# Routed experts run as one pipeline, and mixture stages whose shared units go first with expert choice beside the second unit

## The reference, cut to what matters

```python
# twice (stages a and c): expert choice, each of 8 experts takes its 1024 best tokens
S = sigmoid(xt @ Wg).T;  G, I = top_k(S, 1024);  ex = xt[I]
hid = gelu(einsum('ekh,ehf->ekf', ex, W1) + b1)            # FF = 1024
out = (einsum('ekf,efh->ekh', hid, W2) + b2) * G[..., None]
x = x + 0.5 * zeros.at[I].add(out)
# twice (stages d and f): each token takes 4 of 16 experts out of 2 of 4 groups, and all take the shared part
scores = softmax(x @ gate_w.T);  c = weights of the 4 chosen, 0 elsewhere
y = einsum('tei,eid,te->td', silu(x@w1) * (x@w3), w2, c)   # INTER = 128
z = silu(x @ ws1) * (x @ ws3) @ ws2                        # 2 * 128 wide
x = x + 0.5 * (y + z)
```

## Time and profile before

| what | value |
|---|---|
| time of 3 runs | 4653.36 us median (4644.17 to 4657.75) |
| profiled execution, its own time | 4639.34 us |
| its span | 4637.6 us |
| PE, DVE, ACT, POOL busy | 87%, 59%, 43%, 12% |

### The profile page before, as it was taken

How to read it: one execution, slowest core, us unless ns; L and a number is a source line. 1 busy time by engine, 2 the same in 40 slices (tenths; PEclk the granted TensorE clock), 3 DMA queues, 4 the chain that set the end, 5 groups by cost and what they waited for, 6 DMA issues and landing times. The chain is left out here.

```text
span 4637.6 us, 74096 instructions
## 1 busy us (share of the span) xinstructions
PE 4047.9 (87%) x26222; PEld 3129.6 (67%) x26222; DVE 2729.8 (59%) x5268; ACT 1988.4 (43%) x3960; POOL 566.3 (12%) x428
## 2 busy tenths in 40 slices
PE   4599949989974599968999969999999997799999
PEld 3488835555544588857888856666566664788888
DVE  4544446665645544437777756655666555577777
ACT  1555524544440555512333336555655554133332
POOL 0144321211200144210000000000000000000000
PEclk6699968999995799969999979999999999699999
DMA  3243220000003343220000020000000001000001
GB/s 113 89 93 82 30 57 6 24 20 16 24 25 100 100 85 80 29 56 11 14 10 11 6 77 6 10 11 11 1 10 10 11 6 38 18 11 14 10 14 36
DMA packets 144876, 159.23 MB, mean 34 GB/s; under 512 B 20320, under 2 KB 132704, under 8 KB 144352
## 3 DMA queue, kind: packets, MB, share of 16 engines
q1 hardware_dynamic: 117728, 113.15, 7.5%
q0 software_dynamic: 26880, 42.48, 5.0%
HBM read 105.01 MB, written 50.59 MB: 34 GB/s over the span
## 5 line engine op out<-in xcount | busy, mean ns | idle before, releaser
L1895 ACT ACTIVATE e_prob<-e_s_ps,e_small 128x512 f32<-128x512 f32 x512 | 346.7, 685 | 173.2 <-PE e_t_ps L1785 88.2
L2006 DVE TENSOR_REDUCE e_small<-e_s_ps 128x2 f32<-128x1024 f32 x256 | 313.3, 1224 | 170.8 <-PE e_s_ps L1772 166.6
L1312 ACT ACTIVATE b_pt<-b_t_ps 128x1024 f32<-128x1024 f32 (+3 forms) x256 | 180.9, 706 | 305.0 <-PE b_t_ps L1244 304.0
L1785 PE MATMUL e_t_ps<-const,e_prob 128*128 128x128 f32 x2048 | 267.9, 274 | 9.5 <-ACT e_pt L1884 5.3
L1806 PE MATMUL e_z_ps<-e_pt,e_v 128*64 128x512 f32 x1024 | 275.5, 617 | 0.4 <-DVE e_zf L2086 0.4
L1984 POOL TENSOR_TENSOR e_wide<-e_small,const 128x512 f32<-128x512 f32 x64 | 66.5, 1039 | 1708.4 <-DVE e_small L2079 1708.4
L1785 PEld LDWEIGHTS e_t_ps<-const,e_prob 128*128 128x128 f32 x2048 | 234.1, 141 | 55.8 <-issue 22.5
L1495 DVE TENSOR_REDUCE b_small<-b_s_ps 128x2 f32<-128x1024 f32 (+3 forms) x256 | 209.8, 820 | 85.1 <-PE b_s_ps L1223 81.1
L942 DVE SCALAR_TENSOR_TENSOR d_xs<-d_o_ps,d_coef,d_xs 128x256 f32<-128x256 f32 x576 | 238.1, 476 | 1.3 <-PE d_o_ps L62 1.3
L942 DVE SCALAR_TENSOR_TENSOR f_xs<-f_o_ps,f_coef,f_xs 128x256 f32<-128x256 f32 x576 | 238.1, 476 | 1.3 <-PE f_o_ps L62 1.3
L60 PE MATMUL f_h_ps<-f_x_hi,f_w_hi 128*128 128x512 f32 x576 | 227.5, 395 | 0.0
(11 more groups left out here) (540 smaller groups left out, 11757.0 us busy)
## 6 DMA issues: line engine op xcount, KB each, us to landing
ae_raw<-w_dram SPq DMA_DIRECT2D x16, 1024.0 KB
ce_raw<-w_dram SPq DMA_DIRECT2D x16, 1024.0 KB
d_raw<-m_dram SPq DMA_DIRECT2D x54, 128.0 KB, 2.2
f_raw<-m_dram SPq DMA_DIRECT2D x54, 128.0 KB, 2.2
b_xs<-x_dram SPq DMA_DIRECT2D x9, 512.0 KB, 3.8
ar_xs<-x_dram SPq DMA_DIRECT2D x8, 512.0 KB, 9.3
x_dram<-ar_xs SPq DMA_DIRECT2D x8, 512.0 KB, 7.6
rows_dram<-ar_xn POOLq DMA_DIRECT2D x8, 512.0 KB, 4.7
```

What stands on the lines that cost most here:

```text
L1312: act.activation(pt[:, kt % 2, a, :, 0:width], t_ps[:, :, 0:width], ACT.Exp).then_inc(p_ready, 1)
L1785: last = pe.transpose(t_ps[:, h, kt * P:(kt + 1) * P], prob[:, bank_of(s) + h, kt * P:(kt + 1) * P], ident)
L1895: act.activation(prob[:, at], s_ps[:, at], ACT.Exp, bias=nmx[:, at:at + 1], accum_out=sums[:, buf, h * QT + s:h * QT + s + 1]).then_inc(p_ ...
L2006: dve.tensor_reduce(nmx[:, at:at + 2], s_ps[:, at:at + 2], AX.X, ALU.max, negate=True).then_inc(mx_ready, 1)
```

## The change

**Experts.** down follows its up by two steps (LAG = 2), across experts too, so `h_hi` and `h_lo` have 4 buffers and the x parts 2. The next expert's transposes are spread over steps 8, 10, 12 and 14, its weights are split in 8 pieces of twice the size, and the last half's bias and gate come in the third step of the next expert. Gathers signal in pairs, and GpSimd issues the gather of expert e+2 between the two scatters of expert e.

**Mixture.** The unit order is rotated: the two shared units, whose coefficient is the constant 0.5, are units 0 and 1. Transposes and logits of group g run between the steps of unit 0, out of the second half of `o_ps`; the logits are copied to SBUF. The choice of experts is cut in eight parts, and DVE runs one behind each step of unit 1. The low part `h_lo` is made on GpSimd instead of DVE in all 144 steps. The weights of unit 1 are loaded behind the tokens.

```diff
 def ffn0_experts(nc, tag, rows, x_out, w1, b1, w2, b2, const, idx):
+        LAG, RING = 2, 4
+        SPLIT_AT = (2, 3, 4, 5, 7, 9, 11, 13)
+        TURN_AT = (8, 10, 12, 14)
...
+            def gather_next(e):
+                gp.wait_ge(t_ready, e * PAIRS)
+                gp.wait_ge(gates_done, e)
+                gather(e)
...
             for e in range(E0):
-                body(e, e + 1 < E0)
-            gp.wait_ge(added, E0 * 16 * CC)
+                scatter(e, 0)
+                if e + 2 < E0:
+                    gather_next(e + 2)
+                scatter(e, 1)
...
             def body(e, b, more):
                 for n in range(N):
                     up(e, b, n)
-                    if n >= 1:
-                        down(e, b, n - 1)
-                if more:
-                    transposes(e + 1)
-                down(e, b, N - 1)
+                    if n >= LAG:
+                        down(e, b, n - LAG)
+                    elif later(e):
+                        down(e - 1, 1 - b, N + n - LAG)
+                    if isinstance(e, int) and e == 0 and n in (0, 2):
+                        transposes(0, 2 + n // 2)
+                    if more and n in TURN_AT:
+                        transposes(e + 1, TURN_AT.index(n))
...
                     act.activation(hid[:, n % 2], h_ps[:, n % 2], ACT.Gelu, bias=b1_sb[:, b, f:f + 1]).then_inc(hid_ready, 1)
-                    if more:
-                        split_w(e + 1, 1 - b, n)
...
+                    if more and n in SPLIT_AT:
+                        split_w(e + 1, 1 - b, SPLIT_AT.index(n))
...
+                    if more and n in TURN_AT:
+                        split_x(e + 1, 1 - b, TURN_AT.index(n))
+                    if n == LAG and later(e):
+                        scale_y(e - 1, 1 - b, 1)
+                    if n == FC + LAG:
                         scale_y(e, b, 0)
...
 def moe(nc, tag, x_in, x_out, gate_w, w1, w3, w2, const):
...
             def weights(u, b):
+                at = (u + E1) % UNITS
...
             def down(b, g, first):
                 n = first + g
                 pe.wait_ge(hid_lo, n + 1)
-                if isinstance(n, int) and n < 2:
-                    pe.wait_ge(soft_in, 2)
-                else:
+                head = isinstance(n, int) and n < NG
+                if head and n:
+                    pe.wait_ge(o_used, n)
+                elif isinstance(n, int) and NG <= n < NG + 2:
+                    pe.wait_ge(o_used, NG)
+                    pe.wait_ge(lg_out, 1)
+                elif not head:
                     pe.wait_ge(o_used, n - 1)
...
+            for k in range(KC):
+                transposes(0, k)
+            for g in range(NG):
+                more = g + 1 < NG
+                if more:
+                    transposes(g + 1, 0)
+                else:
+                    pe.wait_ge(x_lo_done, NG * KC)
+                logits(g)
+                if more:
+                    transposes(g + 1, 1)
+                up(0, g, 0)
+                if g >= 1:
+                    down(0, g - 1, 0)
...
+        @block.gpsimd
+        def _(gp):
+            def unit(b, first, u, more):
+                for g in range(NG):
+                    gp.wait_ge(hid_hi, first + (g + 1))
+                    gp.tensor_tensor(h_lo[:, g % 2], hid[:, g % 2], h_hi[:, g % 2].bitcast(F32), ALU.subtract).then_inc(hid_lo, 1)
...
-                dve.wait_ge(hid_hi, n + 1)
-                dve.tensor_tensor(h_lo[:, g % 2], hid[:, g % 2], h_hi[:, g % 2].bitcast(F32), ALU.subtract).then_inc(hid_lo, 1)
...
+            normalise(0)
+            split_w(0, 0)
+            normalise(1)
+            for k in range(KC):
+                split_x(0, k)
+            for g in range(NG):
+                if g + 1 < NG:
+                    for k in range(KC):
+                        split_x(g + 1, k)
+                if g + 2 < NG:
+                    normalise(g + 2)
+                step(0, g, 0, 1)
+                if g >= 1:
+                    add(g - 1, 0, 0)
...
             def unit(b, first, u, more):
                 for g in range(NG):
                     step(b, g, first, u + 1 if more else None)
                     if g >= 1:
                         add(g - 1, first, u)
-                    elif not isinstance(u, int) or u > 0:
+                    else:
                         add(NG - 1, first - NG, u - 1)
+                    if isinstance(u, int) and u == 1:
+                        choose(g)
```

More of the change, by code:

```diff
@@ L437, in loads_of, with later, over_experts @@
         def loads_of(e, b):
-            return e * 8 + (8 if b else 16)
+            return 16 * (e // 2 + 1) if isinstance(e, int) else e * 8 + (8 if b else 16)
+        def later(e):
+            return not isinstance(e, int) or e > 0
+        def over_experts(eng, body):
+            body(0, 0, True)
+            with eng.Fori(0, E0 // 2 - 1) as i:
+                body(i * 2 + 1, 1, True)
+                body(i * 2 + 2, 0, True)
+            body(E0 - 1, 1, False)
         @block.sync
@@ L545, in _, with split_w @@
+                    if isinstance(e, int) and e == 0 and n in (0, 2):
+                        transposes(0, 2 + n // 2)
+                    if more and n in TURN_AT:
+                        transposes(e + 1, TURN_AT.index(n))
+            for j in range(PAIRS // HALF):
+                transposes(0, j)
+            over_experts(pe, body)
+            for n in range(N - LAG, N):
+                down(E0 - 1, 1, n)
         @block.scalar
         def _(act):
[L547 to L549 removed]
+            def split_w(e, b, m):
+                if m == 0:
+                    act.wait_ge(w_in[b], 2 * loads_of(e, b))
@@ L561, in body, with scale_y @@
+            def scale_y(e, b, g):
+                act.wait_ge(y_sum, e * HALF + (g + 1))
+                for t in range(GT):
+                    last = act.activation(y[:, g, t], y[:, g, t], ACT.Copy, scale=gates[:, b, g * GT + t:g * GT + t + 1])
+                last.then_inc(y_ready, 1)
             def body(e, b, more):
-                act.wait_ge(b1_in[b], (e // 2 + 1) * 16 if isinstance(e, int) else loads_of(e, b))
+                act.wait_ge(b1_in[b], loads_of(e, b))
                 for n in range(N):
@@ new lines, in body @@
+                    if isinstance(e, int) and e == 0 and n in (0, 2):
+                        split_x(0, 0, 2 + n // 2)
+                    if more and n in TURN_AT:
[3 more added lines that the diff above has]
+                    if n == FC + LAG:
+                        scale_y(e, b, 0)
+            for m in range(WS):
+                split_w(0, 0, m)
+            for j in range(PAIRS // HALF):
+                split_x(0, 0, j)
@@ L639, in _ @@
-            for n in range(N):
-                split_w(0, 0, n)
-            split_x(0, 0)
-            dve.wait_ge(b2_in, 16)
-            body(0, 0, True)
-            with dve.Fori(0, E0 // 2 - 1) as i:
-                body(i * 2 + 1, 1, True)
-                body(i * 2 + 2, 0, True)
-            body(E0 - 1, 1, False)
+                    dve.tensor_tensor(h_lo[:, n % RING], hid[:, n % 2], h_hi[:, n % RING].bitcast(F32), ALU.subtract).then_inc(hid_lo, 1)
+                    if more and n in SPLIT_AT:
+                        split_w(e + 1, 1 - b, SPLIT_AT.index(n))
@@ L650 @@
+                    if more and n == FC + 1:
+                        take_gates(e + 1, 1 - b)
+            for m in range(WS):
+                split_w(0, 0, m)
+            for j in range(PAIRS // HALF):
+                split_x(0, 0, j)
+            dve.wait_ge(b2_in, 16)
+            over_experts(dve, body)
+            add_b2(E0 - 1, 1, 1)
 E1, TOPK, EG, TOPG = 16, 4, 4, 2
-UNITS = E1 + 2
+SHARED = 2
+UNITS = E1 + SHARED
 INTER = 128
@@ L747, in logits @@
                 last.then_inc(lg_ready, 1)
-            pe.wait_ge(c_loaded, 16)
-            pe.wait_ge(gw_ready, 2)
-            transposes(0)
-            for g in range(NG):
-                if g + 1 < NG:
-                    transposes(g + 1)
-                logits(g)
             def up(b, g, first):
@@ new lines, in _ @@
+            row_stats(dve, st, lambda g: dve.wait_ge(loaded[g], 16), xs, stats, mean, var, rstd, tmp, half)
+            normalise(0)
+            split_w(0, 0)
+            normalise(1)
+            for k in range(KC):
+                split_x(0, k)
+            for g in range(NG):
+                if g + 1 < NG:
+                    for k in range(KC):
+                        split_x(g + 1, k)
+                if g + 2 < NG:
+                    normalise(g + 2)
+                step(0, g, 0, 1)
+                if g >= 1:
+                    add(g - 1, 0, 0)
```

380 lines of the change are left out of this document (180 added, 200 removed).

## The result

| | before | after |
|---|---|---|
| median, 4 runs each on one chip | 4655.56 us (4644.17 to 4661.78) | 4510.9 us (4506.45 to 4514.31) |
| profiled execution, its own time | 4639.34 us | 4506.45 us |
| its span | 4637.6 us | 4504.7 us |

The changed kernel takes 0.9691 of the time before, 95% interval 0.967 to 0.9713. Forecast were 4536 us, in a range of 4500 to 4585.

The account below looks back on a forecast made before the run. PE, busy 87% of the span, was taken as the bound, so gains come from its gaps or clock. Experts -87.3 and mixture -30, together -117.5, make 4639.3 into 4521.8; with 14.0 to the median 4536 us, range 4500 to 4585.

Parts of the forecast that it names:

- the forecast's own range: Whole kernel: the prediction's own mechanism holds, 4515 to 4560 us, chance 0.50.
- the transposes stay, 2.3 us an expert: Experts' body: transposes still cost 2.3 us an expert but stand in the stream, within a body of 380.2 us.
- The heavy third step: Experts' third step: ACT also has a weight piece and scaling, 3.6 us against 2.82, so ACT is 2.9 us late.
- the cover: Experts: the lag hides the rest; without it up to 3 us in each of 7 experts, 21 a stage.
- Slack: Mixture step: with the low part on GpSimd at 1.25 us, 0.7 us is left before down, where 1.27 was.
- So nothing in the 595 us: Stage d's 595 us with PE the bound: low part on GpSimd changes nothing there, 0.5 us at the stage's end.
- Unit 0, 80 us forecast: Mixture unit 0: eight rounds at 9.5 us, clock falling in most, plus prologue; bounds 66 always full, 123 never.
- Unit 1, +9 us forecast: Mixture unit 1: the choice behind its 8 steps adds 6 us, with DVE and GpSimd collisions +9 us.
- The clock stays up in unit 0: Rival, mixture unit 0: the clock stays up, 14 us less a stage, 4510 us; chance 0.10.
- The mixture gives nothing: Rival, mixture: clock falls in all eight rounds and unit 1 collisions are doubled, 4566 us; chance 0.20.
- A new wait in the experts: Rival, experts: heavy third step or late gather costs 3 us twice an expert, 4580 us; chance 0.12.
- GpSimd late in every step: Rival, mixture: h_lo at 2.37 us comes 0.42 to 0.5 late in 272 steps, 136 us, 4672 us; chance 0.05.

Follow-up runs that it names:

- the two kernels that take them out: Changed kernel with down one step behind up: 4566.74 us; changed kernel with all four pairs of transposes behind an expert's last up, lag kept: 4552.53 us.
- Two kernels: Changed kernel with coef padded to 18 columns: 4487.94 us; kernel before with mixture buffers moved 6016 bytes: 4634.31 against 4621.31 us.
- the mixture alone: Kernel before with only the mixture stages changed and the experts as before: 4631.59 us, ratio 0.9962 to the kernel before.
- the padding: Changed kernel with coef padded from 17 to 18 columns, buffers 6144 bytes further on than before the change: 4487.94 us, ratio 0.9707 to the kernel before.
- no GpSimd beside it: Changed kernel with the mixture's low part back on VectorE in all 144 steps: 4525.81 us, ratio 0.9732 to the kernel before.
- The doubled low part: Changed kernel with GpSimd making each low part twice, first into a tile nobody reads: 4638.66 us, ratio 0.9968 to the kernel before.

## Why the prediction was right, and where its terms were off

**How right it was.** The sum came out 25 us better than forecast. The direction and the main mechanism held: PE's gaps and clock were the bound, and both halves of the change gave their time there. The sizes were off in both directions, more often to the cautious side: the experts by 8.3 us in all and units 0 and 1 by some 5 each in a stage, against 4.8 a stage too little for the steady units. So the median missed the forecast's own range, and lies in the stated one because that took in the rivals.

**Experts, -87.3 forecast, -95.6 found.** The head was sized right: 6.9 us forecast from first weight copy to first `up`, 6.82 found (the copy itself came 2.8 us later, with the stage ahead of it). The body was 380.2 forecast and 376.4 found. The step is 2.82 us as before; the mis-sized term is "the transposes stay, 2.3 us an expert". A step with a pair takes 3.26 us, 0.44 more, so 1.76 an expert; seven times the difference of 0.54 are the 3.8 us. The period is 46.9 us, not 47.4. The heavy third step, which I had feared, brings no wait at all. The lag and the spreading both carry the gain, by the two kernels that take them out; the prediction gave the cover to the lag alone.

**Low part on GpSimd.** 1.25 us taken, 1.31 found, just above the range of 1.19 to 1.29. Slack 0.7 taken, 0.86 found. The conclusion, no wait in the steady units, holds. It is worth 11.8 us in units 0 to 2, which the prediction had not singled out, and costs 1.2 in the last one. There the prediction had 0.5; the wait is 0.6 longer and the clock takes the rest.

**"So nothing in the 595 us": wrong by 0.04 us a step.** The step took 4.22 and not 4.18 us, some 5 us a stage, because the new small tensors moved the weights and buffers by 6016 bytes. Two kernels show it, one from each side. Nothing in my reading of the change looked at where tensors lie.

**Unit 0, 80 us forecast, 74.7 found.** The rounds were forecast at 9.5 us with the clock falling in most. They take 7.74 with the clock up, and 9.33 and 9.30 where it falls; it falls in three of eight, in stage f too (the third of these has no transposes and takes 8.45). The forecast of 7.8 at full clock was right; wrong was how often it falls, and for how much of a round: a long one costs 1.6 us over a short one, where I had 2.8. How often the clock is lost is not fixed by the kernel: in stage d of the mixture alone the first two rounds took 9.21 and 8.79 us, and 8.16 and 7.74 here, with the same code. What decides it stays open.

**Unit 1, +9 us forecast, +3.9 found, and +1.9 in unit 2** (over 33.44; with the padding 3.8 and 1.6). The choice was sized by its window, 18.7 us less 0.8. Its work is less, and part of it falls into unit 2, for which the prediction had nothing: DVE is busy 12.0 us longer in unit 1 and 3.2 in unit 2 than in unit 3, 15.2 in all; with no GpSimd beside it, by the same three rows, 9.3 and 4.6, 13.9. The wait for the exponential and the table was sized right, 2.61 us of DVE idle where 2.6 were forecast. The collisions were 0.4 us a step, 3.2 in all, in the forecast. Found are three, of 0.66 to 0.68 us each, two in unit 1 and one in unit 2: 2.0 us. The Trainium skill, SBUF — State Buffer, section "SBUF: two separate sides", has a DVE instruction with two SBUF inputs and a GpSimd one that reads SBUF exclude each other for a whole instruction. The trace agrees: line 982 started at 2035.21, GpSimd's subtraction ended at 2036.00, and the instruction ended 0.55 us behind that. The mechanism was right and its price too high, since few instructions of the choice meet GpSimd.

**Sum of the mixture, -30 forecast, -37.1 found.** In stage d, -5.3 for unit 0, -5.1 for unit 1, +1.9 for unit 2, +4.8 for the fifteen units behind and +0.4 at the end make -3.3 of the window, 658.1 us where 661.5 were forecast. The origin came 0.6 us earlier in stage d and 1.7 in stage f, not 1.1.

**From the profile to the median.** Of the 25.1 us by which the median lies under the forecast, 15.4 are these terms (4521.8 forecast for the profiled execution, 4506.45 found). The other 9.7 are the distance from profile to median, which I carried over at 14.0 and which is 4.5 in the changed kernel.

**Rivals.** The clock stays up in unit 0: not so, three rounds lose it. That the time came out at its 4510 is chance: it is the sum of the terms above. The mixture gives nothing: no, though taken alone nearly half of it was lost in stages that it doesn't touch. A new wait in the experts: none. GpSimd late in every step: no. The subtraction is hardly held: most of stage d's 144 take 1.30 us, and the longest, beside a weight split, 1.43. The doubled low part shows what lateness costs.

## What to carry to other kernels

Where a loop ends with work that each engine does for the next round, move that work into the steps and let the consumer lag by one step more; either alone gave a quarter to a half of what both gave. Price small matmuls between dense ones by their own windows, at both clocks, and try the order on the chip, since splitting a run of small ones lost the clock more often here. Where GpSimd takes work from VectorE, look which VectorE instructions read two SBUF tiles beside it, and what waits at the end of the loop, where nothing covers GpSimd's slower instruction. When a new tensor is put in front of matmul operands, look at the steady step's window before and after, and pad if it has moved.

## What the runs showed that I had not expected

Where SBUF operands lie changes the pace of matmuls: buffers 6016 bytes further on made 24 matmuls take 4.22 us in place of 4.18, 6144 bytes did not. Which of the operands matters, and by what rule of addresses, wasn't tried.

A stage that no edit touches changed by 19 us of 1218 in one kernel, which has 12.1 us of "issue" idle time of PE at a line where before has none. In the thirteen other traces stage e is 1212.5 to 1222.1 us. A change measured alone can so be half hidden by a stage it has nothing to do with.

The experts' change may not gain the same on each chip. The kernel before, with its mixture buffers shifted, had expert stages of 432.9 and 432.7 us on the third chip, where the trace of before has 439.8 and 443.5. One period of the shifted kernel at the place of the 53.28 us of the earlier trace rows, then two periods of before that kept the clock:

```profile
230.41:281.39 50.98, 47.74 (x306) 42.66 (x305) 22.93 (x40) 29.49 (x61) 20.81 (x16) 1.00 0.40 84
```

```profile
282.62:334.43 51.81, 48.00 (x306) 42.52 (x305) 22.91 (x40) 29.48 (x61) 20.97 (x16) 1.00 0.38 83
334.43:386.14 51.71, 47.99 (x306) 42.57 (x305) 22.92 (x40) 29.48 (x61) 20.80 (x16) 1.00 0.38 82
```

Within before's own trace a period at 1.00 is some 1.5 us shorter than one at 0.97. The other 0.7 to 0.8 us are mostly a second wait of PE for `h_lo`, 0.5 us long in each of these periods of before, which the shifted kernel's period has not. That the chip makes the difference is not shown, as there is one trace of each. The changed experts have no gap and took 393.8 to 394.1 us with the head as changed, in every trace, whichever the chip.
